# The opening of attention batch 0: score units ahead of the counts, and three waits for `routed` taken apart

## What is computed

```
xn = layernorm(x)                        # x: 16 batches x 512 tokens x 128
q, k = l2norm(xn @ Wq), l2norm(xn @ Wk)  # 16 heads of 8
attn = softmax(mask(8 * q @ k.T));  a = (attn @ (xn @ Wv)) @ Wo
top 2 of 8 experts by softmax(xn @ Wr); gates normalised over the two
f = sum over the two experts: gate * (gelu(xn @ W1[e].T + b1[e]) @ W2[e].T + b2[e])
out = x + a + f
```

## Time and profile before

| | us |
|---|---|
| median of 3 runs | 680.27 (679.78 to 681.35) |
| the profiled execution | 680.41 |
| its span, first to last instruction | 678.7 |
| batch 0 of attention, from its first unit | 90.17 to 117.09 |
| batch 1 | 117.09 to 137.01 |
| batch 2 | 137.01 to 156.37 |
| expert stage | from 254.56 |

### The profile page before, as it was taken

The page is one execution under the profiler, slowest core; times in us unless marked ns, Lnnn a source line. Parts: engine busy times, 40 slices in busy tenths (PEclk is TensorE's granted clock), DMA queues, the critical chain, the costliest instruction groups (busy, mean ns, idle before and its releaser), DMA issues. The chain is left out here.

```text
span 678.7 us, 21454 instructions
## 1 busy us (share of the span) xinstructions
PE 615.8 (91%) x7417; PEld 411.7 (61%) x7417; DVE 465.7 (69%) x1312; ACT 449.9 (66%) x689; POOL 418.0 (62%) x584
## 2 busy tenths in 40 slices
PE   2877558999999999999999999999999999999965
PEld 2755323444444438999999999999984444444423
DVE  7799986766676776445545446777566687878826
ACT  3999546888888884444444444444449888888854
POOL 6355627778777787775600027677737777677771
PEclk9899968999999999999999999999999999999989
DMA  5997685655445578855432335444536375556621
GB/s 160 297 288 228 185 248 111 109 108 104 115 115 118 125 126 199 206 143 143 108 88 71 73 88 120 112 115 118 120 78 104 84 137 116 121 124 139 122 68 32
DMA packets 186592, 89.36 MB, mean 132 GB/s; under 512 B 115456, under 2 KB 176032, under 8 KB 186400
## 3 DMA queue, kind: packets, MB, share of 16 engines
q1 hardware_dynamic: 178192, 70.70, 44.7%
q0 software_dynamic: 8336, 17.84, 9.8%
HBM read 30.17 MB, written 32.24 MB: 92 GB/s over the span
## 5 line engine op out<-in xcount | busy, mean ns | idle before, releaser
L812 ACT ACTIVATE prob<-psum 128x1536 f32<-128x1536 f32 x192 | 267.2, 1453 | 64.0 <-PE psum L922 62.2
L822 ACT ACTIVATE prob<-psum,prob 128x256 f32<-128x256 f32 x284 | 117.5, 471 | 132.2 <-PE psum L1062 129.3
L648 POOL DMA_INDIRECT rows<-slot_y,idx x128 | 130.4, 1019 | 46.1 <-issue 27.2
L650 POOL DMA_INDIRECT slot_x<-rows,slots x128 | 128.2, 1001 | 36.1 <-issue 30.4
L954 PE MATMUL psum<-prob,v 128*18 128x448 f32 (+3 forms) x2048 | 137.9, 388 | 8.6 <-POOL prob L664 8.6
L664 POOL TENSOR_SCALAR_AFFINE_SELECT prob<-prob 128x384 f32<-128x384 f32 (+2 forms) x224 | 104.8, 477 | 62.6 <-ACT prob L812 60.5
L1074 PEld LDWEIGHTS psum<-prob 128*128 128x128 f32 x1136 | 137.8, 192 | 3.6
L1074 PE MATMUL psum<-prob 128*128 128x128 f32 x1136 | 138.1, 275 | 0.0
L1062 PE MATMUL psum<-xs,prob 128*128 128x256 f32 x568 | 134.8, 380 | 0.6 <-DVE xs L1468 0.4
L1062 PEld LDWEIGHTS psum<-xs,prob 128*128 128x128 f32 x568 | 102.5, 190 | 12.4 <-DVE xs L1468 0.6
L954 PEld LDWEIGHTS psum<-prob,v 128*18 128x18 f32 x2048 | 48.8, 98 | 97.0 <-issue 75.9
(11 more groups left out here) (159 smaller groups left out, 661.3 us busy)
## 6 DMA issues: line engine op xcount, KB each, us to landing
slot_y<-xs SPq DMA_DIRECT2D x71, 128.0 KB
xs<-in_L_attn_x SPq DMA_DIRECT2D x16, 256.0 KB, 4.1
prob<-in_L_ffn_W SPq DMA_DIRECT2D x16, 256.0 KB, 3.6
xn_rows<-prob SPq DMA_DIRECT2D x16, 256.0 KB, 2.7
xn_cols<-xts SPq DMA_DIRECT2D x16, 256.0 KB, 3.0
xt<-xn_cols SPq DMA_DIRECT2D x16, 256.0 KB
rows<-xn_rows SPq DMA_DIRECT2D x16, 256.0 KB, 3.5
out<-acc SPq DMA_DIRECT2D x15, 256.0 KB
```

The costliest lines, as they stand in the source:

```text
L648: pool.indirect_dma_start(rows[:, j, c, t, :], None, done, where).then_inc(moved[j], 16)
L650: pool.indirect_dma_start(slot_x, where, halves_of_rows[:, j, 0, t, :], None).then_inc(moved[j], 16)
L812: act.activation(prob[:, KEPT[k], :], score[k % 2], ACT.Exp, scale=SCALE / UP ** 2)\
L822: act.activation(hs[:, s, c, :], psum[:, 2 * s + c // 2, (c % 2) * FT:(c % 2 + 1) * FT], ACT.Gelu, bias=ws[:, s, B1C + c:B1C + c + 1]).the ...
```

## The change

Nothing is computed differently, except that `ps_o` is no longer cleared. The parts:

- `routed` is split in three. `counts_read` is raised when VectorE has copied the counts out of `ps_o`, and `weigh(0, 0, 0)` waits for it. `ranks_read` is raised two operations into the rank arithmetic, when `ps_pc` has been read, and `project(1, 0)` waits for it. GpSimd's moves still wait for `routed`.
- TensorE does unit 0 of batch 0 ahead of the count matmuls, and units 1 and 2 between the counts and the rank matmuls. The rest of batch 0 has an order of its own, `first_batch`: projections of batch 1 after units 4, 8, 9 and 11.
- VectorE copies the biases (`bt_ready`) ahead of the last selection and the shared values behind it, and evacuates the first half of batch 0 after two of four preparations.
- GpSimd issues the padding after the mask of unit 1.
- ScalarE takes the square roots of batches 10 and 11 ahead of the last squares.

```diff
@@ GpSimd, body
-                if known(b, 0):
-                    pad_last_tiles()
                 for k in range(UN):
                     mask(b, k)
+                    if known(b, 0) and k == 1:
+                        pad_last_tiles()
@@ ScalarE
+            roots(NB // 2 - 3)
             for s in range(2):
                 squares(NB // 2 - 1, 1, s)
-            for i in range(NB // 2 - 3, NB // 2):
+            for i in range(NB // 2 - 2, NB // 2):
                 roots(i)
@@ TensorE, project and weigh
                     if i == 0 and known(b, 1):
-                        pe.wait_ge(routed, 1)
+                        pe.wait_ge(ranks_read, 1)
...
                     if known(b, 0):
-                        pe.wait_ge(routed, 1)
+                        pe.wait_ge(counts_read, 1)
@@ TensorE, ahead of the batches
+            pe.wait_ge(bt_ready, 1)
+            pe.wait_ge(proj_evac, TB)
+            scores(0, 0, 0)
+
             pe.wait_ge(selected, T // ST)
...
             mm.then_inc(counted, 1)
+            scores(0, 0, 1)
+            scores(0, 0, 2)
             pe.matmul(ps_pc, before[:], flat_both, start=True, stop=False)
...
-            pe.wait_ge(bt_ready, 1)
-            pe.wait_ge(proj_evac, TB)
+
+            def first_batch():
+
+                for k in range(3, UN):
+                    scores(0, 0, k)
+                    if k == 3:
+                        weigh(0, 0, 0)
+                    elif k == 4:
+                        project(1, 0)
+                    elif k in (5, 6, 7):
+                        weigh(0, 0, k - 4)
+                    elif k == 8:
+                        project(1, 1)
+                    elif k == 9:
+                        weigh(0, 0, 4)
+                        project(1, 2)
+                    elif k == 10:
+                        weigh(0, 0, 5)
+                        weigh(0, 0, 6)
+                    else:
+                        project(1, 3)
+                        weigh(0, 0, 7)
@@ VectorE
-            for c in range(TOPK):
-                select(T // ST - 1, c)
             dve.wait_ge(btr_done, 1)
...
+            for c in range(TOPK):
+                select(T // ST - 1, c)
+            share_values(0, 0)
...
             stepped(dve.tensor_copy(counts[:], ps_o[:, 0:2 * E].rearrange("p (c e) -> p c e", c=2)))
+            dve.sem_inc(counts_read, 1)
...
             stepped(dve.tensor_tensor(at_rank, ranks, of_halves(begins[:, 0:2]), ALU.add))
+            dve.sem_inc(ranks_read, 1)
...
-            dve.memset(ps_o, 0.0).then_inc(r_step, 1)
-            dve.wait_ge(r_step, next_step())
             dve.sem_inc(routed, 1)
@@ VectorE, body
-                if known(b, 0):
-                    share_values(0, 0)
...
                     prepare(b + 1, 1 - par, 1, second)
+                    if known(b, 0):
+                        evacuate(0, 0)
                     prepare(b + 1, 1 - par, 2, second)
```

25 lines of the change are left out of this document (13 added, 12 removed).

## The result

| | before | changed |
|---|---|---|
| median of 14 runs each (us) | 680.06 (678.03 to 681.35) | 682.67 (681.15 to 684.41) |
| ratio, 95% interval | | 1.004 (1.0028 to 1.0051) |
| the profiled execution | 680.41 | 681.78 |
| its span | 678.7 | 680.1 |
| first unit of batch 1 / of batch 2 | 117.09 / 137.01 | 116.04 / 139.63 |

The changed kernel is **slower by 2.7 us** (1.9 to 3.5 by the interval). The two terms of the sum do not: the start of batch 1 came 1.4 us sooner than forecast, and the half clock cost 2.1 us more. That the sum fits is in part luck.

The account below looks back on a forecast made before the run. TensorE's own work was taken to bound the kernel from batch 1's first unit of scores. A 0.3 us later start plus 1.6 us of half clock gave +1.9 on the profiled 680.41; forecast median 682.1 us, range 679.3 to 684.2.

Parts of the forecast that it names:

- The two terms of the sum: Batch 1 starting 0.3 us later, plus 1.6 us for half clock inside batch 1: together +1.9 us.
- Part 1: Opening of batch 0: unit 0 at 87.1, counts at 89.1, padding address at 94.9, `routed` at 100.5 to 101 us.
- Part 2: Loosened waits: TensorE's stalls of 3.11 us (first projection of batch 1) and 2.47 us (second half's value product) both go.
- Part 3: GpSimd after unit 5's mask: late padding holds its moves until 102.7, unit 8's mask ends at 109.4, TensorE idles 2 us.
- the padding lands later than `routed`: GpSimd ahead of its first move: padding lands at 102.2 to 102.9, `routed` comes at 100.5 to 101 us.
- TensorE is idle for 2 us there: Value product `1A1`: TensorE reaches it at 107.4 but needs unit 8's mask, which ends at 109.4 us.
- the shared queues of the prediction: Padding transfer: it overlaps the residual's load for about 3 us instead of 5.4, so takes 7.0 us instead of 7.8.
- the marks that I had set: Trace tests: first move not before 102; forecast wrong if moves start at 100.5 or batch 1's first unit before 116.
- Rival (d): Padding takes its full 7.8 us whatever the load does: +0.8 to +1, 683.1 us; chance 0.10.
- Part 4: Batch 1's last projection ends at 111.6, 5.8 us more to batch 1: 0.3 us later start, almost 4 us idle TensorE.
- Part 5: Clock: the 3.8 us idle stretch ahead of batch 1 brings half clock into batch 1, costing 1.6 us.
- rival (a): Half clock also follows the idle time before `1A1`: +1.8 us, 683.9 to 684.1; chance 0.18.

Follow-up runs that it names:

- e5: Changed kernel with units 0, 1 and 2 put back behind the count and rank matmuls, all else staying changed; median 683.2 us.
- e2: Changed kernel with only unit 0 moved behind the counts, so units 0 to 2 stand between count and rank matmuls; median 682.19 us.
- e9: Kernel of e6 with unit 0 ahead of the counts and units 1 and 2 ahead of the ranks, old TensorE order behind; median 681.71 us.
- e10: Kernel of e6 with batch 1's scales (two VectorE operations) moved into VectorE's wait for the counts; median 676.01 us.
- e6: Kernel of e3 plus the change's VectorE and ScalarE edits ahead of batch 0 (biases, shared values, square roots); median 677.46 us.
- e12: Changed kernel with GpSimd's eight moves of batch 0 spread, one behind each mask from unit 5 and two behind unit 11's; median 681.37 us.
- e1: Changed kernel with four matmuls nobody reads added behind batch 0's last value product, in TensorE's idle stretch ahead of batch 1; median 680.42 us.
- e4: Changed kernel with only batch 1's last projection moved, from behind unit 11 to ahead of `1A1`; median 679.47 us.
- e3: Kernel before with only `routed` split in three and the clearing of `ps_o` dropped, every engine's order kept; median 678.22 us.

## Why the prediction came out right, and which steps did not

**Part 1** held: unit 0 at 86.82 (87.1), counts at 88.86 (89.1), the padding's address ready at 94.87 (94.9). `routed` was put at 100.5 to 101 and came near 101.7, since the ranks took 6.7 us instead of 5.6. Two steps account for it. The first ran beside GpSimd's masks of units 2 and 3, the second beside that of unit 4 (98.32 to 98.86). First VectorE's rows of the changed kernel, then GpSimd's:

```profile
97.02 1.40 DVE L1353 TENSOR_TENSOR rows<-rows,logits 128x512 f32<-128x512 f32 x1
98.46 0.94 DVE L1355 TENSOR_TENSOR rows<-hot,rows 128x512 f32<-128x512 f32 x1
...
96.40 1.48 POOL L664 TENSOR_SCALAR_AFFINE_SELECT prob<-prob 128x384 f32<-128x384 f32 x2
```

The two masks took 0.74 us each there, where 0.54 is usual for the form. In the kernel before, the same two steps took 0.69 us each, and masks ran near them as well. There GpSimd's timeline shows a mask that took long, 0.94 us where the same form takes 0.54:

```profile
94.24 0.69 DVE L1323 TENSOR_TENSOR rows<-rows,logits 128x512 f32<-128x512 f32 x1
94.97 0.69 DVE L1325 TENSOR_TENSOR rows<-hot,rows 128x512 f32<-128x512 f32 x1
...
96.57 0.94 POOL L664 TENSOR_SCALAR_AFFINE_SELECT prob<-prob 128x384 f32<-128x384 f32 x1 [0.75 <-ACT prob L812]
```

So steps of both engines seem to grow where they lie beside each other; no run separates the cause. I had costed the ranks by their old length and not asked what GpSimd now does beside them.

**Part 2** held: the stall of 3.11 us went, and 0.46 us are left of the one of 2.47. A wait that I named nowhere came instead, the second projection for VectorE's first preparation: 1.69 us.

**Part 3: two steps failed, "the padding lands later than `routed`" and "TensorE is idle for 2 us there", before `1A1`.** GpSimd's timeline of the changed kernel:

```profile
95.17 1.21 POOL L623 DMA_INDIRECT slot_x<-acc,pad_at  x1 [0.70 <-DVE pad_at L1339]
...
101.95 0.98 POOL L650 DMA_INDIRECT slot_x<-rows,slots  x1 [1.74 <-DVEq L1361]
...
107.78 0.55 POOL L664 TENSOR_SCALAR_AFFINE_SELECT prob<-prob 128x384 f32<-128x384 f32 x1
```

The padding was issued at 95.17 as forecast and landed after 6.0 us, not 7.0, at 101.2; VectorE was done with the ranks at 101.57. The profile puts the first move's wait of 1.74 us down to VectorE, that is to `routed`, and the move started at 101.95 instead of 102.7; unit 8's mask ended at 108.33 instead of 109.4. TensorE came to `1A1` at 108.14 instead of 107.4, since it had waited 1.69 us for the first preparation and 0.46 for the transpose, and so stood there for 0.24 us, not 2. (By the prediction's own instants, 100.6 and 102.7, GpSimd's wait would also have been 2.1 us and not the 2.6 that it gives.)

`routed` and the padding came nearly level, however. In e5 VectorE had finished the ranks at 97.83, and the first move started no sooner. VectorE's last step on the ranks in e5, then GpSimd's padding and first move:

```profile
97.14 0.69 DVE L1357 TENSOR_REDUCE slots<-rows 128x64 int32<-128x512 f32 x1
...
95.61 1.21 POOL L623 DMA_INDIRECT slot_x<-acc,pad_at  x1 [0.63 <-issue]
...
101.97 0.98 POOL L650 DMA_INDIRECT slot_x<-rows,slots  x1 [1.06 <-ACT prob L813]
```

There the padding landed at 101.2 as well (after 5.6 us), and from the landing to the move it was 0.8 us. The same 0.7 to 0.8 us lie between them in e2, e9 and e10, where the ranks were done sooner too, and in the changed kernel. So the prediction was right that the padding holds GpSimd (in e5 by itself, here level with `routed`), and wrong in the instant.

What set that instant was not the issue. In the eleven kernels for which the profile gives both, the padding landed 2.4 to 2.6 us after the load of the residual (1.2 in e6), whether it had been issued at 93.23 (kernel before: load 98.6, padding 101.0), at 93.81 (e10: 98.7 and 101.2) or at 95.17 (98.7 and 101.2). This fits the shared queues of the prediction, which had taken 0.8 us off for them where 1.8 went; no run moves the load alone, so it stays a reading.

By the marks that I had set, the moves did start before 102, if only by 0.05 us, and batch 1 missed the mark "before 116" by 0.04. Rival (d) did not occur: the landing took 7.8 us before and 6.0 now, though VectorE's rank arithmetic ran beside the issue both times, and for longer now (6.7 against 5.6 us). The Trainium skill ("SBUF — State Buffer", the trap named "DVE blocks DMA") has such a DMA wait for its descriptors while VectorE holds the shared port. Whether the rank arithmetic holds that port no row here shows; the shorter landing beside the longer arithmetic does not bear it out.

**Part 4: mechanism right, term mis-sized.** -1.05 instead of +0.3 us. Of the 1.35 between them about 1.0 is the start of `1A1` from part 3 (108.38 instead of 109.4, so that the last projection ended at 110.61 instead of 111.6), and 0.37 the way from there to batch 1: 116.04 - 110.61 = 5.43 instead of 5.8. The path to the last projection was another than forecast: without any wait for the mask `1A1` would have started 0.24 us sooner, and e12, which takes that wait away, has batch 1 only 0.6 us sooner by its own opening. What came later than I had it was TensorE itself, behind VectorE's first preparation. The idle stretch was 3.50 us (forecast 3.8), and the last thing to land was the transposing DMA (ScalarE was through with its exponentials at 111.3).

**Part 5: mechanism and place right, size wrong.** I took 1.6 us from a dip of 3.5 us in the earlier trace rows; the dip lasted some 10 us and batch 1 took 3.67 us more. The failing step is "what this idle stretch costs is what the last one cost". That no dip came before `1A1` was forecast, and rival (a) did not occur.

So the forecast of +1.9 came close to the measured +2.6 by two errors of opposite sign, and that is luck. Had only the start been right, the forecast would have been 0.6; had only the clock been right, 4.0. The experiments support the mechanism (e1 for the clock, e4 for the projection) more firmly than the sum did. (The terms also add up to 682.2, not 682.1, if the 0.14 is taken off 682.3.)

Open: why the half clock lasts now 3.4, now 6.8, now 10 us; why the opening starts up to 1.4 us sooner or later from one execution to another, at the same order of work ahead of it; which part of e9's 4 us lies behind batch 1; whether e6 gains over e3; what the clearing of `ps_o` is worth in e3.

## What to carry to other kernels

When a stall is removed in front of a stage that one engine bounds, ask for the last thing that stage waits for, and whether the change moved its producer later; the idle time then gathers right at the stage's start. An idle stretch of TensorE there can cost more than its length (here 3.50 us of it were followed by 3.67 us lost to the half clock), so put work with long latency behind it (here the projection with its preparation and transposing DMA) as early as it can go, and keep TensorE busy up to the start, if need be with useless matmuls. Work moved ahead of a short step on which a long chain of another engine hangs can be paid for by the whole chain (e9). And a transfer that is issued sooner need not land sooner: ask what else the queues carry.

## What the runs showed of the hardware

- **The half clock after an idle stretch has no fixed price.** In the kernel before, idle stretches of 3.11 and 2.47 us were each followed by about 3.5 us at 1.2 GHz. In the changed kernel 3.50 us were followed by 10 us, in e4 2.89 us by 6.8 us, in e12 4.41 us by 6.8 us, in e5 1.90 us by 3.4 us, and in e10 2.46 us by none. TensorE was busy for nearly all of each of these stretches. The 1.69 us of the changed kernel at 103.64 were followed by none either. The idle length alone does not tell which it will be. The Trainium skill ("TensorE: Matmul & The Clock Gate", Part 1) says that the monitor runs freely and that the point of change varies; the different outcomes agree with that, but no run here varies the phase alone.
- **Filling idle time keeps the clock**: 2.85 us of useless matmuls in a stretch of 3.6 us (e1) left it at 1.00 through all of batch 1.
- **VectorE and GpSimd seem to slow each other**: a 128x512 step with two inputs took 1.40 and 0.94 us beside GpSimd's masks where 0.69 is usual, and a mask 0.94 us beside VectorE's ranks where 0.54 is usual. That is read from where the rows stand, not shown by an experiment.
- **The landing of the same indirect DMA** (the padding) took 5.6 to 8.9 us from kernel to kernel, but ended 2.4 to 2.6 us after another transfer, the load of the residual, in ten of eleven kernels, whatever the instant of its issue (93.2 to 96.2).
- **GpSimd's wait for a landed DMA**: the first move started 0.7 to 0.8 us after the padding's landing where `routed` had come before (e2, e5, e9, e10).
